# The softmax shift of each batch: transposed and spread through a DRAM scratch, in place of a diagonal multiplied by ones

## The reference

```python
# x: (8, 56, 128), ctx: (8, 1500, 128), mask: (8, 56); 16 heads of 64
h = layernorm(x)
q, k, v = heads(h @ Wq), heads(ctx @ Wk), heads(ctx @ Wv)
dots = einsum('bhnd,bhmd->bhnm', q, k) * SCALE
dots = dots - (1 - mask)[:, None, :, None] * 1e6
x = x + merge(softmax(dots) @ v) @ Wout + bout
tokens = layernorm(x)                       # 8 experts, one for each batch of 56 tokens
x = x + gelu(tokens @ w1 + b1) @ w2 + b2
```

## Time and profile before

| what | value |
|---|---|
| median of 3 runs | 385.91 us (384.51 to 385.98) |
| the profiled execution, its own time | 386.91 us |
| its span | 385.0 us, granted clock of TensorE 0.989 of full |
| busy: PE, DVE, ACT, POOL | 367.7, 284.7, 255.0, 116.4 us |
| chain of waits by engine | PE 79%, DVE 11%, issue 5%, DMA 2%, ACT 1% |

### The profile page before, as it was taken

The page is one execution under the profiler, slowest core; times in us unless marked ns, Lnnn a source line. Parts: engine busy times, 40 slices in busy tenths (PEclk is TensorE's granted clock), DMA queues, the critical chain, the costliest instruction groups (busy, mean ns, idle before and its releaser), DMA issues.

```text
span 385.0 us, 5782 instructions
## 1 busy us (share of the span) xinstructions
PE 367.7 (96%) x1713; PEld 280.6 (73%) x1713; DVE 284.7 (74%) x456; ACT 255.0 (66%) x334; POOL 116.4 (30%) x125
## 2 busy tenths in 40 slices
PE   6899999999999999999999999999999999999794
PEld 6667777777677877777777777777777876787563
DVE  5798667978797679878797679787788678343653
ACT  3455577697669476696679466787678456958421
POOL 1520573246224350246034341336142420022000
PEclk9899999999999999999999999999999999999988
DMA  6685269329832772359834591269546450376100
GB/s 241 219 171 168 46 118 209 82 86 167 196 80 80 146 174 52 84 126 238 193 86 121 96 211 38 82 149 257 126 109 139 90 107 6 109 144 120 24 2 6
DMA packets 30622, 47.10 MB, mean 122 GB/s; under 512 B 2011, under 2 KB 21371, under 8 KB 30608
## 3 DMA queue, kind: packets, MB, share of 16 engines
q0 software_dynamic: 9936, 27.40, 36.4%
q1 hardware_dynamic: 20672, 19.52, 16.5%
HBM read 24.59 MB, written 0.23 MB: 64 GB/s over the span
## 4 chain that ended last, share of the span: by engine, by line
PE 79%; DVE 11%; issue 5%; DMA 2%; ACT 1%; SPq 1%; DVEq 0%
PE ps_s L439 26%; PE ps_a L479 22%; PE ps_x L496 10%; PE ps_a L472 7%; PE ps_x L529 4%; DVE chunk_max L899 2%; PE ps_a L416 2%; PE ps_x L549 2%; DMA ctxt_raw<-in_ctx_t 2%; DVE ex_lo L895 2%; DVE shift_diag L910 1%; DVE ex_sum L889 1%; PE ps_x L453 1%; PE ps_x L558 1%; PE ps_x L511 1%
## 5 line engine op out<-in xcount | busy, mean ns | idle before, releaser
L899 DVE TENSOR_REDUCE chunk_max<-ps_x 128x1 f32<-128x500 f32 x168 | 110.8, 676 | 32.3 <-PE ps_x L496 29.2
L697 ACT ACTIVATE ex_all<-ps_s 125x896 f32<-125x896 f32 x96 | 88.1, 918 | 48.5 <-PE ps_s L439 46.6
L479 PE MATMUL ps_a<-ex_all,ctx_sb 125*128 125x448 f32 x248 | 110.9, 540 | 0.0
L715 ACT COPY ps_s<-shift_row 125x896 f32<-125x896 f32 x94 | 85.7, 911 | 12.5 <-DVE shift_row L1036 10.0
L496 PE MATMUL ps_x<-ctxt_hi,qk_hi 128*128 128x500 f32 x168 | 82.0, 490 | 4.7 <-DVE chunk_max L899 3.6
L1213 POOL DMA_DIRECT2D ex_all<-ex_all x48 | 42.4, 884 | 119.6 <-ACT ex_all L697 116.4
L439 PE MATMUL ps_s<-qk_hi,ctxt_hi 128*125 128x448 f32 x192 | 76.4, 479 | 0.0
L479 PEld LDWEIGHTS ps_a<-ex_all,ctx_sb 125*128 125x128 f32 x248 | 46.2, 189 | 17.2 <-issue 12.8
L439 PE MATMUL ps_s<-qk_lo,ctxt_hi 128*125 128x448 f32 x192 | 54.8, 367 | 0.0
L439 PE MATMUL ps_s<-qk_hi,ctxt_lo 128*125 128x448 f32 x192 | 54.8, 366 | 0.0
L439 PEld LDWEIGHTS ps_s<-qk_hi,ctxt_hi 128*125 128x125 f32 x192 | 35.9, 187 | 24.5 <-issue 22.8
(11 more groups left out here) (108 smaller groups left out, 402.7 us busy)
## 6 DMA issues: line engine op xcount, KB each, us to landing
ex_all<-ex_all POOLq DMA_DIRECT2D x48, 448.0 KB, 4.8
ctxt_raw<-in_ctx_t SPq DMA_DIRECT2D x8, 750.0 KB, 6.0
ctx_sb<-in_ctx SPq DMA_DIRECT2D x8, 750.0 KB
ctxt_hi<-in_ctx_t POOLq DMA_DIRECT2D x21, 250.0 KB, 3.0
w_sb<-in_w SPq DMA_DIRECT2D x4, 512.0 KB, 4.9
w_sb<-in_w SPq DMA_DIRECT2D x8, 256.0 KB, 7.0
ex_all<-in_wq_t SPq DMA_DIRECT2D x2, 256.0 KB, 3.8
ex_all<-in_wk_t SPq DMA_DIRECT2D x2, 256.0 KB, 4.9
```

The source lines that it names most:

```text
L479: mm = nc.tensor.matmul(ps_a[:, c, 0:CH], ctx_sb[0:MT, u, t, :], ex(t)[0:MT, c * CH:(c + 1) * CH], start=(slot == 0), stop=(slot == TM - 1))
L697: nc.scalar.activation(half(ex(t)[0:MT, :]), src, ACT.Exp, scale=SCALE).then_inc(ex_ready, 1)
L715: nc.scalar.copy(ps_s[0:MT, t % 2, :, 0:CH], half(shift_row[0:MT, b.parity, :])).then_inc(seeded, 1)
L899: nc.vector.tensor_reduce(chunk_max[:, k, t:t + 1], filled()[:, 0:MC], AX.X, ALU.max).then_inc(job_free, 1)
```

## The change

`MAX_AT` is changed in one entry a row: the job at (9, 0) goes, in the even row to a second job at (2, 2), in the odd row to (4, 0). All maxima are done at (8, 2). The shift arithmetic on VectorE moves from (10, 0) to (8, 3), and the diagonal goes away except for batch 0's own. TensorE transposes `row_max` (128 x 7) at (9, 0) into a bank, 7 x 128, with the identity as the moving operand; VectorE scales it into `shift_of_tile` at the same place. SP stores that to a row of a scratch in DRAM, waits for it, and loads the row back with a broadcast to all 128 partitions of `shift_row`. ScalarE's seed waits for this load. SP's queue gets these two transfers between the loads of `ctxt_raw` and `ctx_sb`; the load of `ctx_sb` for the second batch of a round now stands behind the store of the pair's output and the weights.

```diff
     MAX_AT = [
+        [(1, 0), (1, 1), (1, 2), (2, 0), (2, 1), (2, 2), (2, 2), (4, 0), (4, 1), (4, 2), (5, 0), (5, 1), (5, 2),
+         (6, 0), (6, 1), (6, 2), (7, 0), (7, 1), (7, 2), (8, 0), (8, 2)],
...
-    FIRST_SHIFT_AT, SHIFT_AT = (0, 1), (TM - 2, 2)
+    FIRST_SHIFT_AT, SHIFT_AT = (0, 1), (TM - 3, 0)
...
+        shift_of_tile = sb("shift_of_tile", [QT, P])
+        shift_kept = nc.dram_tensor("shift_kept", (2, Q), F32, kind="Internal").ap()
...
+            def spread_shift(b, drained):
+
+                sp.wait_ge(job_free, drained)
+                sp.dma_start(shift_kept[b.parity:b.parity + 1, :].rearrange("a (t q) -> (a t) q", q=P), shift_of_tile[:, :]).then_inc(shift_kept_in, 16)
+                sp.wait_ge(shift_kept_in, b.at(16, 0))
+                sp.dma_start(shift_row[:, b.parity, :], shift_kept[b.parity:b.parity + 1, :].to_broadcast([P, Q])).then_inc(shift_in[b.parity], 16)
...
             with sp.Fori(0, ROUNDS - 1) as i:
-                load_batch(Batch(i, 3))
-                load_batch(Batch(i, 4))
-
-                store_pair(i, i * ROUND_JOBS + FIRST_JOBS + ROUND_JOBS)
+                before = i * ROUND_JOBS + FIRST_JOBS
+                load_ctxt(Batch(i, 3))
+                spread_shift(Batch(i, 2), before + PLAIN_JOBS)
+                load_ctx(Batch(i, 3))
+                load_ctxt(Batch(i, 4))
+                spread_shift(Batch(i, 3), before + (ROUND_JOBS - 1))
+
+                store_pair(i, before + ROUND_JOBS)
                 load_experts(i + 1)
+                load_ctx(Batch(i, 4))
...
+            def shift_by_tile(b):
+                bank = job()
+                pe.wait_ge(shift_ready, b.at(1, 1))
+                nc.tensor.transpose(bank[0:QT, 0:P], row_max[:, 2, :], ident[:, :]).then_inc(job_ready, 1)
+
...
                     if prepare and at == SHIFT_AT:
-                        pe.wait_ge(shift_ready, b.later(1).at(1, 1))
-                        shift_jobs()
+                        shift_by_tile(b.later(1))
...
-                            act.wait_ge(job_free, jobs.value())
+                            act.wait_ge(shift_in[b.later(1).parity], shift_landed(b.later(1)))
...
+            def shift_drained(b):
+
+                if b.i is not None or b.off > 1:
+                    dve.wait_ge(shift_in[1 - b.parity], shift_landed(b.later(-1)))
+                nc.vector.tensor_scalar(shift_of_tile[:, :], filled()[0:QT, 0:P], 1.0 / SCALE, None, ALU.mult).then_inc(job_free, 1)
+
...
                     if prepare and at == SHIFT_AT:
-                        shift_copies(b.later(1))
+                        shift_drained(b.later(1))
...
-                    if prepare and at == (TM - 2, 0):
+                    if prepare and at == (TM - 4, 3):
                         shifts(b.later(1))
```

More of the change, by code:

```diff
@@ L150, in xattn_ffn @@
     assert all(len(m) == QT * KM and FIRST_SHIFT_AT < m[0] and m[-1] < (TM - 2, 0) for m in MAX_AT)
-    FIRST_JOBS = 2 + 2 * QT * KM + 2 + 4 + 2
-    ROUND_JOBS = 2 * (QT * KM + 2 + 2) + 4
+    FIRST_JOBS = 2 + 2 * QT * KM + 2 + 4 + 1
+    PLAIN_JOBS = QT * KM + 2 + 1
+    ROUND_JOBS = 2 * PLAIN_JOBS + 4
     with ExitStack() as stack:
@@ L244, in xattn_ffn @@
         qk_hi_ready, qk_lo_ready = sem("qk_hi_ready"), sem("qk_lo_ready")
+        shift_kept_in = sem("shift_kept_in")
+        shift_in = [sem("shift_in_even"), sem("shift_in_odd")]
         shift_ready, seeded = sem("shift_ready"), sem("seeded")
@@ L268, in ex, with maxima_at @@
             return ex_all[:, t if t < CHAINS else CHAINS + (t - CHAINS) % RING, :]
+        def maxima_at(b, at):
+            return [n for n, place in enumerate(MAX_AT[b.parity]) if place == at]
         def ctx_split(b):
@@ L281, in added_by_dma, with shift_landed @@
             eng.wait_ge(ex_added[t % CHAINS], b.at(16 * adds, 16 * (t // CHAINS)))
+        def shift_landed(b):
+            return b.at_every_other(16, 16 * b.parity)
         def half(t):
@@ L354, in _ @@
             load_experts(0)
-            load_batch(Batch(None, 2))
+            load_ctxt(Batch(None, 2))
+            spread_shift(Batch(None, 1), FIRST_JOBS)
+            load_ctx(Batch(None, 2))
             with sp.Fori(0, ROUNDS - 1) as i:
-                load_batch(Batch(i, 3))
-                load_batch(Batch(i, 4))
-                store_pair(i, i * ROUND_JOBS + FIRST_JOBS + ROUND_JOBS)
-                load_experts(i + 1)
-            load_batch(Batch(None, B - 1))
-            store_pair(ROUNDS - 1, FIRST_JOBS + ROUNDS * ROUND_JOBS)
+                before = i * ROUND_JOBS + FIRST_JOBS
[5 more added lines that the diff above has]
+                store_pair(i, before + ROUND_JOBS)
+                load_experts(i + 1)
+                load_ctx(Batch(i, 4))
+            before = FIRST_JOBS + (ROUNDS - 1) * ROUND_JOBS
+            load_ctxt(Batch(None, B - 1))
+            spread_shift(Batch(None, B - 2), before + PLAIN_JOBS)
+            load_ctx(Batch(None, B - 1))
+            spread_shift(Batch(None, B - 1), before + ROUND_JOBS - 1)
+            store_pair(ROUNDS - 1, before + ROUND_JOBS)
             load_experts(ROUNDS)
@@ L576, in jobs_at @@
                         sum_jobs(b.later(-1))
-                    if prepare and at in MAX_AT[b.parity]:
-                        k, t = divmod(MAX_AT[b.parity].index(at), QT)
+                    for n in maxima_at(b, at) if prepare else ():
+                        k, t = divmod(n, QT)
                         if t == 0:
@@ L795, in iteration @@
                         if t + 2 == TM:
-                            jobs.n = FIRST_JOBS if first else jobs.n + 2
-                            act.wait_ge(job_free, jobs.value())
+                            jobs.n = FIRST_JOBS if first else jobs.n + 1
+                            act.wait_ge(shift_in[b.later(1).parity], shift_landed(b.later(1)))
                         seed(b.later(1), t + 2 - TM)
@@ L861, in _ @@
             jobs = new_jobs()
-            steps = Tally(2 * (3 + 1) + 3 + 2 + 1, ROUNDS)
+            steps = Tally(2 * (2 + 1) + 3 + 2 + 1, ROUNDS)
             drained = [None]
@@ L907, in shifts @@
                                                     op0=ALU.mult, op1=ALU.add))
-                step(nc.vector.scalar_tensor_tensor(out=row_max[:, 2, :], in0=row_max[:, 1, :], scalar=-1.0, in1=pen,
-                                                    op0=ALU.mult, op1=ALU.add))
+                negated = nc.vector.scalar_tensor_tensor(out=row_max[:, 2, :], in0=row_max[:, 1, :], scalar=-1.0, in1=pen,
+                                                         op0=ALU.mult, op1=ALU.add)
+                if b.i is not None or b.off > 0:
+                    negated.then_inc(shift_ready, 1)
+                    return
+                step(negated)
                 nc.vector.tensor_tensor(shift_diag[:, :, :],
@@ L1030, in xn_transposed @@
                                       filled()[:, 0:(end - first) * P]).then_inc(job_free, 1)
+            def shift_drained(b):
+                if b.i is not None or b.off > 1:
+                    dve.wait_ge(shift_in[1 - b.parity], shift_landed(b.later(-1)))
+                nc.vector.tensor_scalar(shift_of_tile[:, :], filled()[0:QT, 0:P], 1.0 / SCALE, None, ALU.mult).then_inc(job_free, 1)
             def shift_copies(b):
-                wait(dve, seeded, b.at(TM, -TM - 2))
                 for c in range(2):
@@ L1055, in drain @@
                             drain_sum(b.later(-1), c)
-                    if prepare and at in MAX_AT[b.parity]:
-                        max_part(*divmod(MAX_AT[b.parity].index(at), QT))
+                    for n in maxima_at(b, at) if prepare else ():
+                        max_part(*divmod(n, QT))
                     if pair is not None:
@@ L1228, in iteration @@
                     if b.off == 0 and t == FOLD_AT[-1][0] + 2:
-                        pool.wait_ge(job_free, FIRST_JOBS - 2 - sum(at > FOLD_AT[-1] for at in MAX_AT[0]))
+                        pool.wait_ge(job_free, FIRST_JOBS - 1 - sum(at > FOLD_AT[-1] for at in MAX_AT[0]))
                         nc.gpsimd.memset(att_n[:, :, :], 0.0).then_inc(att_n_ready, 1)
```

## The result

The changed kernel takes 391.44 us (median of 4 runs, 388.54 to 394.27) against 385.21 (382.52 to 385.98) for the kernel before: ratio 1.0167, 95% interval 1.0123 to 1.0210. It is slower by 1.7%. The forecast was 386.9 with a range up to 391.0. The profiled execution is the slowest of the four, 394.27 us.

The account below looks back on a forecast made before the run. TensorE, busy 96% of the span, was taken as the bound. Terms -5.50 + 0.84 + 1.28 + 4.35 = +0.97 us, carried over to the median of 385.91, gave 386.9 us, called no change; 8-in-10 range 383.4 to 391.0.

Parts of the forecast that it names:

- The removal: TensorE, step 10: the two shift matmuls and their wait for shift_diag go, 5.50 us together over seven batches.
- 6.47 in the forecast: Added on TensorE at (9, 0): transpositions 0.84 us, waits 1.28 us in four plain batches and 4.35 in three pair batches.
- the transfers' sum: SP's store and broadcast of the shift: 5.4 us with hand-overs and busy engines, so shift_row is in time by 0.2.
- The second rival: Slower: the way through the scratch makes shift_row late, from 5.6 us in plain batches on; about 390 us, chance 0.28.
- the rival at 6.4 us: The second rival's halfway case: shift_row 0.8 us late in four plain batches, 390.1 us.
- 6.8 us by the forecast: Pair batches: time left for the shift's transfers, from its copy done to when shift_row is needed.
- the prediction's own sign of being wrong: Wrong if the transposition waits under 0.5 us in pair batches, or a batch's first scores wait for ScalarE.
- The first: Rival, faster: the three long pair-batch waits at (9, 0) do not come; 383.5 us, chance 0.22.
- The third: Rival: VectorE falls behind where the maxima were put, 0.3 us a batch; 389.0 us, chance 0.08.
- the moved maxima: Job from (9, 0) to (2, 2) or (4, 0): counted at nothing, 0 to 0.3 us a batch possible, 2 us in all.

Follow-up runs that it names:

- e1: Changed kernel, but the broadcast reads a row of the context instead of the scratch, without waiting for the store: 384.27 us, ratio 0.9984.
- e2: Changed kernel with the accumulating transfers of steps 6 to 8 cut from 896 to 32 columns: 385.93 us, ratio 1.0018.
- c1: The changed kernel run again with nothing altered: 390.86 us, ratio 1.0162.
- e3: Kernel before with only the new places of the maxima, diagonal and shift as they were: 383.11 us, ratio 0.9958.
- e4: Changed kernel with the transposition at (9, 2) instead of (9, 0) in the three pair batches: 388.26 us, ratio 1.0094.
- e5: Changed kernel with the shift's store and broadcast ahead of the next ctxt_raw load in SP's queue: 392.51 us, ratio 1.0227.
- e6: Changed kernel with the alterations of e4 and e5 together: 392.12 us, ratio 1.0196.

## Why the prediction was wrong

**The sizes at TensorE were right or too high.** The removal is complete. The weight load of the transposition waits 1.43 and 0.33 us where 1.45 and 0.32 were forecast. In TensorE's queue this costs less than I summed: in the pair batch the group before starts at 150.54 and the one behind at 152.68, 2.14 us, of which two groups at 0.41 would take 0.82, so wait and transposition together cost 1.32 and not 1.57. In the plain batch it is 192.03 - 190.99 - 0.82 = 0.22 and not 0.44. Seven batches: 3 x 1.32 + 4 x 0.22 = 4.8 us against 6.47 in the forecast. With `shift_row` in time the change would be -5.50 + 4.8 = -0.7 us, and e1, which is this, measured -0.6 (0.9984, with no change inside its interval).

**The step that failed is the transfers' sum,** "0.1 + 1.46 + 0.1 + 3.3 + 0.4 = 5.4 us: in time by 0.2". The broadcast took 3.5 us where 3.3 were taken, near enough. The store with its "0.4 for engines that the accumulating transfers still hold" took 2.56 to 3.77 us in the plain batches, 0.6 to 1.8 more than the 1.96 of the sum. By e2 the full engines are the cause in batches 0, 3 and 5, and of about half the excess over 1.2 us in batch 1, whose store keeps 2.30 us without them. Two choices made the term so small. The 1.46 us of the earlier trace rows is from 324.47, in a pair batch, where the kernel before has the engines all but free, a share of 0.10:

```profile
324.50:326.50 2.00, 2.00 (x9) 1.48 (x8) 1.90 (x2) 0.78 (x1) 0.00 (x0) 1.00 0.10 29
```

The share that I took for the plain batch was that of 189 to 191 us, 0.69, while the store was to be issued at 187.0, where the row above it says 1.07. So the earlier trace rows had full engines at the issue; what a small store takes among them stood in none of the rows, and 0.4 us had no row behind it.

**The second rival is what happened, though not for the reason it suspected:** it took the broadcast of one 3.5 KB row to be possibly slow, and it was the store. It was given 0.28, with a bound "from 5.6 us in the four plain batches on". The way from the store's issue to the landing of the broadcast took 7.3, 6.9, 6.1 and 6.3 us in the plain batches (store and 3.5). TensorE waited 2.01, 1.57, 0.79 and 1.06, 5.4 in all, where the rival at 6.4 us charged 0.8 four times. The pair batches have more room, 6.8 us by the forecast, and no wait here (0.2 us once in c1). A wait of a batch's first scores for ScalarE was also the prediction's own sign of being wrong.

The Trainium skill, "DMA: Bandwidth & Descriptors", section "Anatomy of one DMA — SWDGE (gpsimd) path", has a table of fixed and variable time, with about 2.0 us fixed for a transfer that GpSimd issues. Taken as an estimate for this store, which SP issues, it misses both ways: the trace has 1.2 us on empty engines and up to 3.8 on full ones.

**The sum of this execution.** The distance between the first `ctxt_hi` loads of successive batches (a batch's length; the last row is what follows the load for batch 7) gives each term its place. What lies before the first of them, 17.5 to 20.5 us in the ten profiled executions, is left out here.

| stretch | before | e1 | changed | changed - e1 | TensorE's waits for the seed, and more |
|---|---|---|---|---|---|
| batch 0 | 49.84 | 49.56 | 49.75 | 0.2 | |
| batch 1 | 38.64 | 38.22 | 41.94 | 3.7 | 2.01, and 1.7 of clock |
| batch 2 | 44.86 | 45.74 | 47.15 | 1.4 | 1.57 |
| batch 3 | 39.58 | 39.23 | 39.25 | 0.0 | |
| batch 4 | 44.85 | 45.30 | 46.33 | 1.0 | 0.79 |
| batch 5 | 39.65 | 39.26 | 39.27 | 0.0 | |
| rest | 107.1 | 107.0 | 108.9 | 1.9 | 1.06, and 0.9 more before L589 |
| sum | 364.5 | 364.3 | 372.6 | 8.3 | 8.0 |

The 8.3 us between e1 and the changed kernel are thus named but for 0.3. The wait before L589, in the last feed-forward part, was 1.8 us in the kernel before as well, and 0.9 in e1 and 0.4 in c1; it varies and is none of the change. The halved clock was in no step of mine. It is not what makes the kernel slower: c1, without it, is as much slower, and its batch 1 takes 39.72 us instead of 41.94.

**The other rivals.** The first, that the waits at (9, 0) do not come, falls: they came at full length. The third, VectorE falling behind where the maxima were put, falls the other way: I costed the moved maxima at nothing, "between 0 and 0.3 us a batch", and they are worth -1.6 us (e3), since the place they left was in front of the shift. This gain is part of the 5.50 us above and not on top of it.

## What to carry to other kernels

A tiny transfer on the critical path cost here what was queued on the transfer engines at the microsecond of its issue. Its duration is to be read from a transfer issued into the same load, and the share of the engines from the stretch in which it is issued, not from the one behind it. When a change has a part that can be run alone, run it first: here the table of places was the gain and the new mechanism the loss. A shift that starts later costs nothing while the way behind it has room, and a wait once it has none: the later transposition gained 3 us alone (e4) and nothing that can be measured on top of e5 (e6, 392.12 against 392.51).

## What the runs showed of the hardware

- The same store of 3.5 KB from issue to the released next issue: 1.20 to 1.22 us with the engines at 0.01, 2.56 to 3.77 with them at 0.88 to 1.04. The wait on full engines lies ahead of its first packet: 1.62 to 2.38 us after the issue, against 0.74 to 0.78.
- On the loop's first pass the store takes 2.75 us with the engines at 0.04, and 2.30 and 2.88 in e2; one of its seven packets starts when a packet of instructions ends (1.27 and 1.69 us after the issue, where the others are within 0.84).
- 448 KB read from a single 3.5 KB row of memory by all 128 partitions: 3.5 us, hardly slower than the 3.2 us of a 250 KB load. With a 750 KB load beside it, 4.2.
- TensorE's clock at 0.50 (the 1.2 GHz level), 1.7 us lost each time, behind a wait of 2.01 us in one execution and of 1.81 in another (e5); behind waits of 2.30, 1.90 (e6), 1.75 (e5) and 1.57 us it stayed at 1.00.
- A 7 x 128 transposition costs TensorE's queue 0.11 us (152.68 - 152.16 = 0.52 from its start to the start behind the next group, against 0.41 from group to group), near the forecast 0.12; its weight load takes 0.09.
